# Two graph convolutions with layer norms in fp32: conv 2's bias copy and variance take other places, x groups stand between the first block's copies, own rows are fetched there, and each conv's first products come ahead of its second aggregate

## The reference

```python
h = relu(layernorm(x))
h1 = gelu(layer_norm(gcn_conv(h, W1, b1), gamma1, beta1))           # conv 1
h2 = layer_norm(gcn_conv(h1, W2, b2), gamma2, beta2)                # conv 2
x2 = x + gelu(h2 + h)
out = x2 + gcn_conv(relu(layernorm(x2)), W3, b3)                    # conv 3
# gcn_conv(h, W, b) = A @ (h @ W) + b, A = D^-1/2 (edges + I) D^-1/2
```

## Time and profile before

| what | value |
|---|---|
| median of 3 runs | 3188.84 us (3184.24 to 4429.79) |
| profiled execution | 3187.13 us, span in the profile 3185.2 us |
| busy over the span | PE 89%, DVE 78%, POOL 65%, ACT 64% |
| DMA | 890 MB, 279 GB/s over the span |
| prologue, 200 to 300 | DMA share 1.03, 417 GB/s, DVE 81.9 us, PE 27.6 us, clock 0.50 |
| conv 1 starts at | 380.9 us |
| conv 1, 500 to 1100 | PE 600.0 us, DVE 523.6, ACT 422.6, POOL 435.7, DMA share 0.82 |
| conv 2 starts at | 1268.0 us |
| conv 3 starts at | 2306.0 us |
| 2300 to 2350 | PE 33.3 of 50 us, granted clock 0.76 |
| conv 3, 2400 to 3100 | PE 700.0 us, DVE 346.1, ACT 262.0, POOL 401.2, DMA share 0.99 |

### The profile page before, as it was taken

How to read it: one execution, slowest core, us unless ns; L and a number is a source line. 1 busy time by engine, 2 the same in 40 slices (tenths; PEclk the granted TensorE clock), 3 DMA queues, 4 the chain that set the end, 5 groups by cost and what they waited for, 6 DMA issues and landing times. The chain is left out here.

```text
span 3185.2 us, 59158 instructions
## 1 busy us (share of the span) xinstructions
PE 2828.9 (89%) x16428; PEld 2409.9 (76%) x16428; DVE 2477.2 (78%) x5760; ACT 2051.2 (64%) x3083; POOL 2075.0 (65%) x1615
## 2 busy tenths in 40 slices
PE   6022099999999998999999999999699999999999
PEld 3022088888888886888888888888578888888888
DVE  9897588888888887899999999999744554444544
ACT  0565467777777775799999999999733333333333
POOL 0121377777777774888888888888565555555553
PEclk9555599999999999999999999999899999999999
DMA  4999987888888885799999999999799999999996
GB/s 147 384 382 415 344 212 210 219 216 216 213 213 217 217 215 165 269 328 329 334 330 328 330 327 330 330 330 326 253 254 286 289 289 290 285 289 286 288 287 207
DMA packets 304975, 890.16 MB, mean 279 GB/s; under 512 B 67209, under 2 KB 67707, under 8 KB 304922
## 3 DMA queue, kind: packets, MB, share of 16 engines
q1 hardware_dynamic: 189082, 681.53, 61.4%
q0 software_dynamic: 115840, 208.01, 27.7%
HBM read 652.74 MB, written 307.71 MB: 302 GB/s over the span
## 5 line engine op out<-in xcount | busy, mean ns | idle before, releaser
L890 POOL DMA_INDIRECT gathered<-H,idx x826 | 1151.3, 1394 | 516.7 <-issue 238.5
L1278 PE MATMUL out<-Whi,ahi 128*128 128x512 f32 x2832 | 777.1, 396 | 11.3 <-ACT out L973 3.0
L964 ACT ACTIVATE ahi<-agg 128x1024 fp32r<-128x1024 f32 x354 | 360.9, 1019 | 641.8 <-PE agg L1269 641.8
L1278 PE MATMUL out<-Wlo,ahi 128*128 128x512 f32 x2832 | 759.7, 390 | 0.0
L1278 PE MATMUL out<-Whi,alo 128*128 128x512 f32 x2832 | 739.2, 390 | 0.1
L1278 PEld LDWEIGHTS out<-Wlo,ahi 128*128 128x128 f32 x2832 | 532.2, 188 | 115.4
L1278 PEld LDWEIGHTS out<-Whi,alo 128*128 128x128 f32 x2832 | 531.5, 188 | 110.8 <-DVE alo L1089 0.5
L1278 PEld LDWEIGHTS out<-Whi,ahi 128*128 128x128 f32 x2832 | 508.5, 189 | 120.0 <-ACT out L973 27.9
L1081 DVE TENSOR_TENSOR vlo<-gathered,vhi 128x512 fp32r<-128x512 f32 x354 | 243.0, 686 | 316.9 <-ACT vhi L958 316.9
L973 ACT ACTIVATE out<-vec,sqrt_deg 128x512 f32<-128x512 f32 x708 | 457.9, 681 | 15.6 <-PEq L798 9.0
L1089 DVE TENSOR_TENSOR alo<-agg,ahi 128x1024 fp32r<-128x1024 f32 x354 | 428.4, 1210 | 24.9 <-ACT ahi L964 24.7
(11 more groups left out here) (170 smaller groups left out, 3551.1 us busy)
## 6 DMA issues: line engine op xcount, KB each, us to landing
gathered<-H SPq DMA_DIRECT2D x351, 512.0 KB, 6.2
H<-ho SPq DMA_DIRECT2D x250, 512.0 KB, 4.4
x<-in_x_dram SPq DMA_DIRECT2D x165, 512.0 KB, 7.3
X<-x SPq DMA_DIRECT2D x117, 512.0 KB, 8.9
x<-X SPq DMA_DIRECT2D x117, 512.0 KB, 7.5
out_dram<-conv SPq DMA_DIRECT2D x117, 512.0 KB, 9.3
H<-x SPq DMA_DIRECT2D x48, 512.0 KB, 9.7
gathered<-H,idx POOLq DMA_INDIRECT x826, 5.5
```

What stands on the lines that cost most here:

```text
L890: pool.indirect_dma_start(rows, None, H[q][0:end, :], bass.IndirectOffsetOnAxis(ap=idx[p.slot(4)][:, c:c + 1], axis=0), bounds_check=end - ...
L964: nc.scalar.activation(Ahi[p.slot(2)][:, :], Agg[p.slot(2)][:, :], ACT.Copy)\
L1278: m = nc.tensor.matmul(Out[2 * p.slot(2) + j][:, :], a[p.slot(2)][:, c:c + P], w[q][:, f, :], start=False, stop=stop and f == KD - 1, skip ...
```

## The change

Five edits of order, and a wait that is left out:

- Prologue, DVE: more() stands after each of the three pairs of block copies instead of after all, and ahead of each of the three L557. So 16 groups are placed by more() instead of 11.
- Prologue, SP: own rows for pairs 2 and 3 (SelfP[2], SelfP[3]) are fetched with the first two, behind a wait for the last one-hot product (place_used); conv 1 fetches none at its start. The path for general edge lists follows (fetched, reloaded); these inputs don't take it.
- Conv 2, ACT: seed(p+2) stands first in the turn instead of behind gelu(p). In the opening, seed(1) and relu_x of pairs 0 and 1 stand ahead of high(1).
- Conv 2, DVE: x2_var_eps(p-2) stands behind mean_var(p) instead of ahead of it; the wait for rstd_done ahead of the first L1135 is left out where x2_scale has waited for the same value.
- PE, every conv: the first pair's products stand ahead of the second aggregate.

```diff
--- before.py
+++ after.py
@@ -300,8 +300,10 @@
                         load_weights(m)
                 sp.wait_ge(zero_out, 32)
                 sp.wait_ge(w_free, len(WK))
-                for n in range(2):
+                for n in range(4):
                     sp.wait_ge(h0_out[n], 16)
+                    if n == 2:
+                        sp.wait_ge(place_used, NPL // 4)
                     sp.dma_start(SelfP[n], whole(H[0], n, False)).then_inc(self_in.of(Pair(0, n)), 16)
                 sp.wait_ge(vectors_in, 16 * 7)
                 for s in weights_in:
@@ -545,7 +547,7 @@
                     part = bank[c][:, 0:4 * NPAIR].rearrange("p (v n) -> p v n", v=4)
                     nc.vector.tensor_copy(place_i.rearrange("p (n c) -> p c n", c=3)[:, c, :], part[:, 0, :])
                     link(nc.vector.tensor_copy(edge_vals[:, :, c, 0:3].rearrange("p n v -> p v n"), part[:, 1:4, :]))
-                more()
+                    more()
                 link(nc.vector.tensor_scalar(place_lo, place_i, P - 1, None, ALU.bitwise_and))
                 nc.vector.memset(edge_vals[:, :, :, 3:4], 1.0)
                 nc.vector.memset(place_b[:, 3 * NPAIR:NPL], -1.0)
@@ -776,8 +779,8 @@
                 run_pairs(engine, NPAIR + lag, body, lag + 4)
 
             general_sync, general_pool, general_vector, general_tensor = general_sums(q)
-            fetched = 2 if first else 4
-            reloaded = (0, 32, 96, 160)[q + 1]
+            fetched = 4
+            reloaded = 64 * (q + 1)
 
             def general_rows(sp):
 
@@ -1033,21 +1036,21 @@
                             high(p)
                             over_high(p.after(1))
                             if second:
+                                seed(1, p.after(1))
+                                for k in range(2):
+                                    relu_x(k, p.after(k))
                                 high(p.after(1))
                                 over_high(p.after(2))
-                                for k in range(2):
-                                    relu_x(k, p.after(k))
                                 over_high(p.after(3))
-                                seed(1, p.after(1))
                         if second:
+                            if has(known, 2):
+                                seed(of(known, 2), p.after(2))
                             if has(known, -1):
                                 squares(p.after(-1))
                             if has(known, 2):
                                 high(p.after(2))
                             if has(known, 0):
                                 gelu(p)
-                            if has(known, 2):
-                                seed(of(known, 2), p.after(2))
                             if has(known, -2):
                                 relu_x2(of(known, -2), p.after(-2))
                             if has(known, 4):
@@ -1125,7 +1128,8 @@
 
                         m = small[p.slot(4)]
                         if j == 0:
-                            dve.wait_ge(rstd_done.sem, rstd_done.upto(p))
+                            if first or not has(known, -2):
+                                dve.wait_ge(rstd_done.sem, rstd_done.upto(p))
                             dve.wait_ge(cg_done.sem, cg_done.upto(p))
                             if first and (known is None or known >= 2):
                                 dve.wait_ge(h_done.sem, h_done.upto(p.after(-2)))
@@ -1209,16 +1213,17 @@
                             stats(p)
                         if not second and has(known, 5):
                             indices(p.after(5))
-                        if second and has(known, -2):
-                            v = x2_var_eps(p.after(-2))
-                            if not has(known, 0):
-                                v.then_inc(ve_done.sem, 1)
                         if third:
                             if has(known, 0):
                                 result(known, p)
                             return
                         if has(known, 0):
                             mean_var(p)
+                        if second and has(known, -2):
+                            v = x2_var_eps(p.after(-2))
+                            if not has(known, 0):
+                                v.then_inc(ve_done.sem, 1)
+                        if has(known, 0):
                             var_eps(p)
                             centre(p)
                         if first:
@@ -1304,10 +1309,12 @@
                     def body(p, known):
                         if known == 0:
                             aggregate(p)
-                        if has(known, 1):
+                        if has(known, 1) and known != 0:
                             aggregate(p.after(1))
                         if has(known, 0):
                             multiply_second(p, known) if second else multiply(p)
+                        if known == 0:
+                            aggregate(p.after(1))
                     turn(pe, body)
 
             for flag in (idx_made, sv_made, vhi_done, vlo_done, agg_done, hi_done, lo_done, main_done):
```

## The result

The changed kernel takes 3166.59 us (median), the kernel before 3188.57 in the runs beside it: a ratio of 0.9935, 95% interval 0.9919 to 0.9950. That is 22 us, and no change by the 2% that were named. The profiled execution took 3166.59 us, span 3164.8 (3185.2 before). One of five executions on either side ran far longer (3798.7 us at a mean granted clock of 0.73 for the changed kernel, 4429.8 us for the one before), and the ratio leaves these out.

What follows compares the result with a forecast made beforehand. It took DVE, held by POOL's additions, to bound conv 2. Terms -15.1 - 0.5 + 4.9 - 4.5 = -15.2 us, from the median 3188.84, gave 3173.6, said as 3173; 8-in-10 range 3156 to 3191, forecast's own 3165 to 3181.

Steps and rivals of the forecast that it cites:

- Conv 2's variance: Conv 2, DVE: x2_var_eps behind mean_var escapes the hold by POOL's additions; 0.14 us a pair over 108 pairs, -15.1 us.
- DVE alone 8.36: Conv 2: the time a pair would take if only DVE's work set it after the reorder, 8.36 us.
- POOL alone 8.41: Conv 2: the time a pair would need for POOL's gathers, power and additions alone, 8.41 us.
- Rival 3: Conv 2, DVE: POOL's L926 holds the moved L1106 too, 0.09 us a pair later, +10 us; 3199 us, chance 0.08.
- The dropped wait: Conv 2, DVE: omitting the rstd_done wait before the first L1135 gains 0 to 0.05, taken as 0.
- The bias copy: Conv 2, ACT: the earlier copy removes PE's 0.29 us wait but gains 0 in steady state, -0.5 us at the end.
- First products ahead: PE, starts of all convs: first pair's products before the second aggregate cost +0.3, +3.2 and +1.4 us, together +4.9.
- the +1.4: Conv 3's start, PE: products first leave the third aggregate's chain bare, with the clock low until about 2324.3; +1.4 us.
- The other half: Conv 3's start: with second and third aggregates together, PE waits uncovered for the 2.7 us ACT and DVE chain.
- Prologue: Prologue, DVE: more groups between the block's copies fill the dip in DMA share from 160 to 180 us; -4.5 us.
- own rows: Prologue, SP: fetching own rows 2 and 3 early gains 0 us, ends -0.5 and +1.
- Rival 2: Conv 2: POOL's gathers shrink and PE becomes the bound at 8.25 us a pair, -31 us; 3158 us, chance 0.12.

Runs made afterwards that it cites:

- DVE move alone: Kernel before, with only mean_var(p) put ahead of x2_var_eps(p-2) on DVE in conv 2, the rstd_done wait kept: 3173.43 us, ratio 0.9959.

## Why the prediction was right, and where it was off

It said 3173 us and 3156 to 3191; measured were 3166.6, inside that range and inside the forecast's own, 3165 to 3181. Its likeliest time was 6.4 too high. By its terms:

- **Conv 2's variance, -15.1.** The DVE move alone gave -14.7 of block and a pair of 8.41 for the 8.40 said. DVE was the bound, and held by POOL. Of the bounds it gave, "DVE alone 8.36" is what is reached with POOL's additions cut to an eighth (4019 matmuls, 8.36). "POOL alone 8.41" was wrong as a floor: pairs of 8.34 came with POOL's work whole. It had counted the gathers as 1.5 us, and they are 1.38 to 1.41 in the changed kernel. Rival 3 (L1106 held too) falls: L1109 starts under L929 and takes its 0.25 us.
- **The dropped wait, 0.** This is the step that failed. Its argument was that DVE would only wait for ACT's high copy, since the chain L1155, squares, high copy, L1089 is as long; the steps show that right within 0.03 us. It asked only for L1089, and not who else is released by what DVE does in between: L1083 releases POOL's additions, whose end sets how long DVE is held later. Measured -5.8 alone, -5.5 on top of the DVE move: more than the 5.2 by which the whole sum, -15.2, missed the spans' -20.4. The rest of the 6.4 is mostly that it started from a median of 3188.84.
- **The bias copy, 0 in the steady state and -0.5 at the end.** Measured -0.2 alone. PE's 0.29 us a pair of waiting was slack, as said, and a wait of 23.3 us on a page bought nothing when it went.
- **First products ahead, +4.9.** In conv 2 +3.4 for the +3.2 said, and by the mechanism named: the first statistics start 3.9 us later, of which 0.5 comes back. In conv 3 the +1.4 rests on the moment of the clock. The sum had let it rise at the same time as before, 4.2 us into the products. In the profiled execution of the change it rises ahead of them, the first four take 1.18 us, and the cost is some 0.7. In the kernel with aggregates first in conv 2 alone it rises 4.3 us into them, the first four take 2.07 us, and the cost is 1.5 to 2.2. So the sum was right for the moment that it assumed, and that this moment came about in one run and not in the other is chance as far as is known. The change, then the other:

```profile
2299.76 1.18 PE L1283 MATMUL out<-Whi,ahi 128*128 128x512 f32 x4 [1.11 <-ACT ahi L967]
...
2310.01 0.36 PE L1274 MATMUL agg<-sv,vhi 128*128 128x256 f32 x1 [1.84 <-DVE sv L1086]
```

```profile
2296.00 2.07 PE L1283 MATMUL out<-Whi,ahi 128*128 128x512 f32 x4 [1.11 <-ACT ahi L967]
```

  The other half was right: PE then idles 1.84 us before the third aggregate, its chain bare.
- **Prologue, -4.5; own rows, 0.** -5.6 as a mean over kernels, -4.1 in the profiled execution; own rows 0.
- **The sum.** By block -4.1 + 0 - 16.0 - 0.2 = -20.3, the spans' 20.4. By parts in conv 2: -14.7 - 5.5 + 3.4 = -16.8 for 16.0, within the spread. Rival 2 (PE at 8.25) was not reached; by the table of steps DVE and ACT bound the pair in turns, ACT from L1155 to L1089 and DVE from there to the next L1155. No run shortened ACT's part, so that stays argued. That PE is not the common end of the kernels at 8.34 to 8.36 can be worked out: in conv 3, where it is busy throughout, 3838 matmuls in 700 us are 7.30 us for a pair's 40; conv 2's further eight transposes take 0.79 from start to start at their shortest (in the DVE move alone) and its other eight 0.87 for conv 3's 0.79. That makes 8.17, an estimate from these rows, so 0.18 us a pair of PE's busy time in the change is held-up work. In the change it is 0.97 to 1.01 us from the start of those further eight to the next matmul.

## What to carry to other kernels

On the engine that bounds a stage, a small operation that takes three times its usual length is a wait in disguise: look for what ends beside it on the engine that it may share a path with, and put an operation of another kind ahead of it. Where a moved or dropped step is said to gain nothing because the bound engine only waits later, follow also what that engine releases in between: here it was the start of the very work that holds it. A wait on an engine that doesn't bound may be large in the view of waits and worth nothing.

## What was not expected of the hardware

- POOL's additions hold a DVE operation with one tensor and two constants (498 ns for 2 elements) as they hold one with two tensors (489), but not a reduction of the same 2 elements (132).
- Before DVE's L1135 a third wait, for a semaphore long set, cost 0.07 us; a second cost 0.01.
- The recorded length of POOL's gathers isn't fixed. The last of a pair took 1.48 us in before and 1.38 to 1.41 in the changed kernel.
- The moment at which PE's granted clock rises at conv 3's start isn't fixed by the order of the work: in two kernels with the same order there it came 12.9 and 18.2 us after the first bias copy.
- PE's busy time says nothing of slack: it is 699.87 of 700 us at a pair of 8.41 (DVE move alone) and 699.74 at 8.35 (the change).
